# Ordering a tile's main products by PSUM bank within each chunk of the contraction

## What is computed

```
y = einsum('bct,bcd->bdt', x, weights[condition])          # mixing, 32 x 32 per batch
result = einsum('bnd,od->bno', y, W_base) + b_base         # 512 -> 512
probs  = softmax(einsum('bnd,ed->bne', y, W_gate))         # 8 experts
top_p, top_i = top_k(probs, 2); route_w = normalised two-hot
h  = einsum('bnd,erd->bner', y, A)                         # rank 16 per expert, 128 in all
out = x + result + einsum('bner,eor->bno', h * route_w, B)
```

## Time and profile before

| | us |
|---|---|
| median of 3 runs (94.54 to 95.13) | 94.81 |
| the profiled execution | 94.81 |
| its span, first to last instruction | 93.0 |
| TensorE matmul busy in the span | 89.2 (96%) |
| VectorE busy | 65.6 (71%) |
| ScalarE busy | 23.2 (25%) |

### The profile page before, as it was taken

One profiled execution on the slowest core, in us unless ns is written; L12 is line 12 of the kernel. 1 busy time (PEld: TensorE's weight loads), 2 busy tenths in 40 slices (PEclk: granted clock), 3 DMA queues, 4 the chain that ended last, 5 costly groups with the idle time before them and its releaser, 6 DMA issues.

```text
span 93.0 us, 1814 instructions
## 1 busy us (share of the span) xinstructions
PE 89.2 (96%) x642; PEld 85.8 (92%) x642; DVE 65.6 (71%) x229; ACT 23.2 (25%) x55; POOL 15.8 (17%) x29
## 2 busy tenths in 40 slices
PE   6998999999999999999999999999999999999980
PEld 1596999999999999999999999999999999999970
DVE  2887987767675767767675767867675968867660
ACT  2265621312213040312213040312213040311210
POOL 5178103300304040210304040210400000000000
PEclk9999999999999999999999999999999999999999
DMA  1999272422507070322507050332608020302023
GB/s 35 316 307 375 66 217 104 151 93 95 137 1 230 9 210 23 129 104 85 148 0 233 7 204 28 116 120 75 162 7 226 0 113 0 112 8 113 0 113 113
DMA packets 6369, 10.65 MB, mean 115 GB/s; under 512 B 1017, under 2 KB 1625, under 8 KB 6361
## 3 DMA queue, kind: packets, MB, share of 16 engines
q1 hardware_dynamic: 5480, 10.11, 33.2%
q0 software_dynamic: 448, 0.23, 1.2%
q10 hardware_dynamic: 432, 0.20, 0.8%
HBM read 6.35 MB, written 4.19 MB: 113 GB/s over the span
## 4 chain that ended last, share of the span: by engine, by line
PE 87%; DMA 6%; SPq 2%; DVE 1%; ACT 1%; issue 0%
PE main_ps L538 52%; PE y_ps L525 13%; PE main_ps L554 11%; DMA w_raw<-w_all 6%; PE main_ps L616 5%; PE main_ps L622 3%; PE hwT_ps L548 2%; SPq L218 1%; SPq L215 1%; DVE x_sb L506 1%; ACT w_hi L289 1%; PE main_ps L655 0%; SPq L220 0%
## 5 line engine op out<-in xcount | busy, mean ns | idle before, releaser
L538 PE MATMUL main_ps<-w_hi,y_hi 128*128 128x320 f32 x112 | 26.9, 322 | 0.3 <-ACT w_hi L289 0.3
L538 PE MATMUL main_ps<-w_lo,y_hi 128*128 128x320 f32 x112 | 26.7, 320 | 0.0
L538 PE MATMUL main_ps<-w_hi,y_lo 128*128 128x320 f32 x112 | 25.6, 310 | 0.0
L265 POOL DMA_INDIRECT mixw<-cond_w,row_ids x14 | 13.7, 975 | 48.2 <-PE y_ps L525 46.0
L538 PEld LDWEIGHTS main_ps<-w_hi,y_lo 128*128 128x128 f32 x112 | 19.0, 188 | 0.0
L538 PEld LDWEIGHTS main_ps<-w_hi,y_hi 128*128 128x128 f32 x112 | 17.9, 189 | 0.9 <-ACT w_hi L289 0.9
L538 PEld LDWEIGHTS main_ps<-w_lo,y_hi 128*128 128x128 f32 x112 | 18.4, 188 | 0.2
L525 PE MATMUL y_ps<-mix,x_sb 128*128 128x128 f32 x124 | 16.7, 277 | 0.0
L525 PEld LDWEIGHTS y_ps<-mix,x_sb 128*128 128x128 f32 x124 | 15.8, 193 | 0.1
L299 ACT ACTIVATE second<-top 128x1 f32<-128x1 f32 x16 | 4.7, 295 | 42.1 <-DVE top L404 42.1
L431 DVE TENSOR_TENSOR hwT_lo<-hwT_ps,hwT_hi 128x128 fp32r<-128x128 f32 x16 | 4.7, 292 | 13.3 <-ACT hwT_hi L306 13.3
(11 more groups left out here) (67 smaller groups left out, 86.8 us busy)
## 6 DMA issues: line engine op xcount, KB each, us to landing
x_sb<-x SPq DMA_DIRECT2D x16, 256.0 KB, 3.0
out<-x_sb SPq DMA_DIRECT2D x15, 256.0 KB, 2.0
w_raw<-w_all SPq DMA_DIRECT2D x4, 324.0 KB, 5.1
b_raw<-b_lora SPq DMA_DIRECT2D x1, 256.0 KB, 5.8
bias_sb<-bias SPq DMA_DIRECT2D x1, 256.0 KB, 3.7
mixw<-cond_w,row_ids POOLq DMA_INDIRECT x14, 2.5
out<-x_sb ACTq DMA_DIRECT2D x1, 128.0 KB, 1.8
out<-x_sb SPq DMA_DIRECT2D x1, 128.0 KB, 1.8
```

The source lines that it names most:

```text
L265: pool.indirect_dma_start(mixw[:, t, :], None, cond_w, bass.IndirectOffsetOnAxis(row_ids[:, t:t + 1], 0))\
L538: last = pe.matmul(main_ps[t % 2][:, half, 0:n_cols], y, w[:, half * HALF:half * HALF + n_cols], start=i == 0, stop=i == STEPS - 1)
```

## The change

In tiles 2 to 13 the 24 main matmuls get another order. Within a chunk the three operand pairs all go into bank 0 first, and then all three into bank 1. `turn` stands before chunk 1, half 1, that is behind 9 main matmuls and not 8. `lora` stands before chunk 3, half 0, behind 18 as before. Tiles 0, 1, 14 and 15 keep their order. No matmul, load, wait or semaphore is added or taken away; the first matmul into each bank still begins its sum, and the last one of the tile, into bank 1, still signals `main_done`.

```diff
     TURN_AT, LORA_AT = 4, 9
+    TURN_BEFORE, LORA_BEFORE = (1, 1), (3, 0)
...
+            def main_half(t, c, half):
+                n_cols = HALF + half * E
+                for n in range(3):
+                    y, w = operands(c, n, t)
+                    last = pe.matmul(main_ps[t % 2][:, half, 0:n_cols], y, w[:, half * HALF:half * HALF + n_cols],
+                                     start=(c, n) == (0, 0), stop=(c, n) == (CHUNKS - 1, 2))
+                if (c, half) == (CHUNKS - 1, 1):
+                    last.then_inc(main_done, 1)
...
-                for i, (c, n) in enumerate(ORDER):
-                    if t == 1 and (c, n) == (0, 2):
-                        pe.wait_ge(y_lo_ready, 2)
-                    if i == SECOND_MIX_AT and t == 1:
-                        mix_tile(2)
-                    if i == TURN_AT:
-                        turn(t - 1)
-                    if i == LORA_AT:
-                        if t == 1:
+                rank_sums = [main_ps[(t - 1) % 2][:, half, 0:BASE] for half in range(2)]
+                if t == 1:
+                    for i, (c, n) in enumerate(ORDER):
...
+                        main_step(1, i, c, n)
+                else:
+                    for c in range(CHUNKS):
+                        for half in range(2):
+                            if (c, half) == TURN_BEFORE:
+                                turn(t - 1)
+                            if (c, half) == LORA_BEFORE:
+                                lora(t - 1, rank_sums)
+                            main_half(t, c, half)
```

More of the change, by code:

```diff
@@ L600, in _ @@
                     pe.wait_ge(result_ready, t - 1)
-                for i, (c, n) in enumerate(ORDER):
-                    if t == 1 and (c, n) == (0, 2):
-                        pe.wait_ge(y_lo_ready, 2)
-                    if i == SECOND_MIX_AT and t == 1:
-                        mix_tile(2)
-                    if i == TURN_AT:
-                        turn(t - 1)
-                    if i == LORA_AT:
-                        if t == 1:
-                            pe.wait_ge(b_lo_ready, 1)
-                        lora(t - 1, [main_ps[(t - 1) % 2][:, half, 0:BASE] for half in range(2)])
-                    main_step(t, i, c, n)
+                rank_sums = [main_ps[(t - 1) % 2][:, half, 0:BASE] for half in range(2)]
+                if t == 1:
+                    for i, (c, n) in enumerate(ORDER):
+                        if (c, n) == (0, 2):
+                            pe.wait_ge(y_lo_ready, 2)
+                        if i == SECOND_MIX_AT:
+                            mix_tile(2)
+                        if i == TURN_AT:
+                            turn(0)
+                        if i == LORA_AT:
+                            pe.wait_ge(b_lo_ready, 1)
+                            lora(0, rank_sums)
+                        main_step(1, i, c, n)
[7 more added lines that the diff above has]
+                            main_half(t, c, half)
             def side_step(t, i):
```

## The result

The changed kernel takes 95.42 us (median of 22 runs, 94.5 to 96.91) against 94.94 us for the kernel before, measured again beside it (22 runs). The ratio is 1.0049, with a 95% interval of 1.0027 to 1.0071: a loss of 0.3 to 0.7 us. Forecast were 94.9 us, +0.1 us over before. The time is within the forecast's range of 94.2 to 95.8 us and within 1%, but the size of the loss was put too low.

What follows compares the result with a forecast made beforehand. The prediction took TensorE's queue rate to bound the kernel. Its terms, 0.10 us (bank) + 0 (operand) + 0 (turn) on a 93.0 us span, plus 1.8 us around it, gave 94.9 us, range 94.2 to 95.8.

Steps and rivals of the forecast that it cites:

- What bounds the kernel: Middle tiles: only the rate at which TensorE takes its queue, at 2.4 GHz, sets the time; 5.25 us a tile.
- rival B: Main matmuls: alternating banks costs now and the change frees it; 0.15 us faster, 94.7 us; chance beyond that bound 0.07.
- The bank: Main matmuls, tiles 2 to 13: 192 would follow one into the same bank, at +0.5 ns each, +0.1 us.
- The comparison at equal width: At 256 columns, one-bank base_step against alternating lora: the same bank costs between -0.8 and +0.8 ns.
- the other one, across widths: Lines drawn between 256, 324 and 392 columns: same bank 1 to 2 ns dearer, or at most 4 ns.
- Rival A: Main matmuls: writing one bank three times running costs 4 ns for each of 192, 0.77 us, 95.6 us; chance 0.12.
- One sign that I had set for A: Profile after: distances of 150 ns or more within a group of three would show that same-bank writes cost.
- The stationary operand: Main matmuls: 96 more changes between y_hi and y_lo, bounded at 0 to +0.2 us, taken as nothing.
- The place of the turn: Turn 0.147 us later in each tile, hidden by slack; thinnest cover 0.06 us, at turn(13); taken as nothing.
- The sum: Whole kernel: 0.10 + 0 + 0 us on a span of 93.0, giving 93.1, and 94.9 us with 1.8 around it.
- the forecast's own case: Whole kernel: forecast together with no change at all, from -0.15 to +0.4 us; chance 0.78.
- The test that I had set for the tile: Profile after: middle tile stays at 5.25 us within 0.05; prediction wrong if it moves more than 0.08 us.

Runs made afterwards that it cites:

- alt_ops: Kernel before with operand pairs reordered in each chunk: banks alternate, turn behind 8, 20 stationary-operand changes a tile; ratio 1.003, tile 5.276 us.
- probes: Kernel before plus eight 48-matmul blocks on TensorE alone; 1 and 2 alternating banks against one bank, 3 and 4 likewise with stationary operand changing: 7.03 to 7.04 us.
- quiet_tiles: Kernel before plus 15 blocks behind its last matmul, TensorE alone: four whole middle tiles in various orders, then main matmuls alone; 368.11 us.
- new_turn8: Changed kernel with the turn behind 8 main matmuls instead of 9; ratio 1.000, tile 5.261 and 5.263 us in two profiles.
- twelve: Kernel before with all 12 main matmuls of a tile into bank 0, then 12 into bank 1, turn behind 9; ratio 1.004, tile 5.279 us.
- new_mirror: Changed kernel with half 1's operand pairs in order 2, 0, 1, so 12 stationary-operand changes a tile, not 16; ratio 1.001, tile 5.276 us.

## Why the prediction was right, and where it was off

- **What bounds the kernel**: held. TensorE's queue, at the upper clock level, without a wait, before and after. The part of rival B that a lower clock would have carried had nothing to stand on.
- **The bank, +0.5 ns for each of 192 matmuls**: the mechanism is not there. At 320 columns the price is nothing (7.03 against 7.04 us for 48). The changed kernel says the same of itself: by the trace's starts over its 12 tiles, and without the first matmul behind the mixing and behind the turn, a follower into the same bank starts 148.6 ns behind the matmul ahead and one into the other bank 148.5. The comparison at equal width, base_step beside lora, had said so the earlier trace rows; I let the other one, across widths, pull the value up. What it took for a surplus of side_step is a pace that is the same for all the widths in one bank: 146.65 ns at 320 columns is 0.458 ns a column, 180 at 392 is 0.459, 117.5 at 256 is 0.459. Nothing has to be bridged. Rival A falls with it: the loss is real, but alt_ops has nearly all of it without one follower into the same bank. One sign that I had set for A did appear, the nine matmuls behind the turn at 1.36/9 = 151 ns; there, however, the followers into the other bank are as late as those into the same one.
- **The stationary operand, nothing**: held in streams of main matmuls alone, by blocks 1 to 4 of probes and by lines 721 and 722 of quiet_tiles. No run holds it fixed in a whole tile.
- **The place of the turn, nothing**: held for waits. None arose, the idle time of VectorE fell from 0.39 to 0.27 us (0.24 foreseen), and hw of tile 13 ended 0.21 us before the turn loads (81.23 + 0.35 = 81.58 against 81.79 in the timeline), as much as before and not the 0.06 us foreseen. The routing of tile 13 does not hang on finish, as the prediction had it, but on the last main matmul: it starts 0.04 us behind that in both traces, and 0.74 us behind the start of finish before but 0.64 after. That gap took up the delay. In the new order the late turn nevertheless takes 0.018 to 0.020 us a tile more than the early one. That is not a cover that ended: quiet_tiles has it too, with every wait long satisfied.
- **The sum**: +0.1 us was forecast, +0.3 to +0.7 measured. In the prediction's terms, the bank was put at 0.10 us, which no run bears out, and a term of 0.37 us was missing: TensorE's own pace over a whole tile of this order, +0.030 us in each of 12 tiles. That the time lies inside the range owes something to luck. A loss of 0.48 us is beyond the +0.4 us that the forecast's own case reached to, and of the size priced for rival A, whose mechanism is not there; it is A's bound that took the range up to 95.8. I summed edits one at a time, each against its own rows, and assumed that instructions of the same kind and width take the same wherever they stand. They do to 1 ns in 147 on average (147.4 before, 148.6 after), and the queue has 39 matmuls in a tile, 12 times over. The test that I had set for the tile, 5.25 us within 0.05, was met; a loss of 0.4% passes through it.
- **The alternating bank as a cost (rival B)**: falls with blocks 1 and 2. The clock stays at 9 in all 40 slices after too. What the Trainium skill says in "TensorE: Matmul & The Clock Gate", section "A second HAM failure mode: psum-queue depth-cycling", of a kernel that cycles through banks and idles between its groups, with its clock going up and down, does not show in these traces: this kernel cycles through banks without a gap, and its clock stays up.

What is shown: the tile gets longer through the order of TensorE's own queue, with all other engines at rest, and without a wait. A price per follower into the same bank or per change of the stationary operand is not what does it. What is not shown is the mechanism. The sequence of the moving columns moves the pace of the main matmuls alone, and most of the loss appears only with the fp32 mixing, the turn and lora in the queue; no run varies the moving columns, the bank or the operand by itself in a whole tile. Whether the stream collides with anything, and with what, stays open.

## What to carry to other kernels

Where TensorE's queue has no gap, as here, a change of order alone can move the time by some tenths of a per cent (5.247 to 5.281 us a tile over eight orders), though no instruction, wait or byte changes; here rows to 10 ns did not foretell it, and only the length of a repeated stage, averaged over its repeats, shows it. To tell such an effect from a wait or from contention, put copies of the stage behind the kernel's last instruction, where nothing else runs. When a price is read from rows, take the pair of equal width, and distrust a line drawn across widths.

## What the runs showed of the hardware that was not expected

- The mean length of a tile repeats to 0.003 us. Two profiles of the changed kernel have 5.281 us, two of the kernel before 5.250 and 5.247, though their middles begin anywhere from 16.4 to 16.9 us. Over all the kernels here, which have the same work up to there, the middle begins between 15.9 and 18.2 us, and the tile does not follow it. The two profiled executions of new_turn8 differ by 1.86 us, and their middles begin at 17.74 and 15.86 us. So the spread of the runs, over 2 us from 94.35 to 96.72, seems to arise for the larger part ahead of the middle tiles.
- In steady state several orders have tiles of 5.28 or 5.26 us without exception, the kernel before 5.26 and 5.24 in turn or, in another execution, three tiles in 15.74 us. All of these are whole multiples of 20 ns; twelve and new_mirror show no such simple pattern. Why is open.
- Matmuls of 256, 320 and 392 columns into one bank follow on each other at 0.458 to 0.459 ns a column, which is 1.10 cycles of 2.4 GHz. It is no constant: with one set of moving columns for each half, 320 and 328 columns in turn take 14.09/96 = 146.8 ns, or 0.453 ns a column. VectorE and ScalarE at work without pause change this by no more than 0.2 ns at 320 columns. The Trainium skill ("TensorE: Matmul & The Clock Gate", section "Back-to-back issue gap") gives N/2.4 + 2.5 ns as the gap of an isolated matmul and says that this is too much for a stream with weight loads when N is large. By the formula 320 columns would take an estimated 136 ns; the trace of such a stream does not agree, with 146.65.
